# Layer norm of the feed-forward with w1 centred on chip, sums of h and h squared on four column strips, and roots spread over the partitions through HBM

## The reference

```python
h = shift_token(x)                       # features 64..127 come from the token before
q, k, v = split(h @ wqkv)                # 8 heads of 64
q, k = rotary(l2norm(q) * qs, l2norm(k) * ks)
x = x + local_attention(q, k, v) @ wo    # windows of 64 tokens, each looks at its own and the one before
h = shift_token(x)
mu = h.mean(-1); var = h.var(-1)
h = (h - mu) / sqrt(var + 1e-05) * lg + lb
a, g = split(h @ w1 + b1)                # 2 x 341
x = x + (a * gelu(g)) @ w2 + b2
```

## Time and profile before

| | value |
|---|---|
| median of 3 runs | 1300.65 us |
| profiled execution, span | 1302.3 us |
| PE busy | 1259.0 us, 97% |
| ACT busy | 1160.9 us, 89% |
| POOL busy | 1138.8 us, 87% |
| DVE busy | 1093.2 us, 84% |
| granted TensorE clock, mean | 0.999 of full |
| layer 0, attention loop | to about 530 us |
| layer 0, feed-forward and recurrence's gates | to about 690 us |
| layer 1, attention loop | to about 1180 us |
| layer 1, feed-forward and output | to the end |

### The profile page before, as it was taken

One profiled execution on the slowest core, in us unless ns is written; L12 is line 12 of the kernel. 1 busy time (PEld: TensorE's weight loads), 2 busy tenths in 40 slices (PEclk: granted clock), 3 DMA queues, 4 the chain that ended last, 5 costly groups with the idle time before them and its releaser, 6 DMA issues.

```text
span 1302.3 us, 38176 instructions
## 1 busy us (share of the span) xinstructions
PE 1259.0 (97%) x13795; PEld 1007.6 (77%) x13795; DVE 1093.2 (84%) x1883; ACT 1160.9 (89%) x3529; POOL 1138.8 (87%) x840
## 2 busy tenths in 40 slices
PE   7999999999999999899989999999999999999997
PEld 4778888888888887667657888888888888876776
DVE  7888888888888887689878898898888998874777
ACT  5889999999999999777778999999999999998886
POOL 5999999999999988378779999999999999994776
PEclk9999999999999999999999999999999999999999
DMA  5222222222222221010011222222222222110223
GB/s 168 54 63 63 62 62 63 62 63 65 68 66 67 55 62 47 17 54 1 1 29 39 47 46 46 46 47 46 50 48 59 47 46 46 39 38 25 72 75 97
DMA packets 59258, 70.04 MB, mean 54 GB/s; under 512 B 7232, under 2 KB 37376, under 8 KB 59072
## 3 DMA queue, kind: packets, MB, share of 16 engines
q1 hardware_dynamic: 59072, 67.61, 20.8%
HBM read 13.33 MB, written 4.19 MB: 13 GB/s over the span
## 4 chain that ended last, share of the span: by engine, by line
PE 71%; POOL 11%; DVE 6%; issue 6%; ACT 5%; DMA 0%; DVEq 0%; SPq 0%; ACTq 0%; POOLq 0%
PE ps L209 57%; PE ps L272 7%; POOL t L1293 5%; PE ps L285 3%; PE ps L282 3%; ACT P L674 2%; POOL P L1293 2%; POOL hxr L1293 2%; DVE t L1003 2%; POOL side L1323 1%; DVE t L1014 1%; DVE nm L1033 1%; DVE B L1074 1%; DMA norm<-X 0%; ACT sqk L648 0%
## 5 line engine op out<-in xcount | busy, mean ns | idle before, releaser
L674 ACT ACTIVATE P<-ps,nm 128x128 f32<-128x128 f32 x1024 | 363.4, 383 | 0.4
L209 PE MATMUL ps<-wqkv,hT 128*128 128x512 f32 x1152 | 330.1, 427 | 15.7 <-DVE t L1003 12.9
L1293 POOL TENSOR_TENSOR t<-t 128x1024 f32<-128x1024 f32 x128 | 307.0, 2398 | 26.1 <-DVE t L1003 24.3
L1293 POOL TENSOR_TENSOR P<-P,rden 128x512 f32<-128x512 f32 x256 | 289.9, 1143 | 19.3 <-DVE rden L1040 18.1
L209 PEld LDWEIGHTS ps<-wqkv,hT 128*128 128x128 f32 x1152 | 214.5, 188 | 95.8 <-issue 28.0
L1293 POOL TENSOR_TENSOR t<-t,rr 128x1024 f32<-128x1024 f32 x128 | 244.0, 1907 | 19.3 <-ACT rr L657 19.1
L674 ACT ACTIVATION_READ_ACCUMULATOR P<-ps,nm 128x1 f32 x1024 | 229.8, 224 | 0.0
L1014 DVE TENSOR_TENSOR t<-ps,tabl 128x512 f32<-128x512 f32 x256 | 164.1, 683 | 41.8 <-ACT sqk L648 40.6
L1293 POOL TENSOR_TENSOR hxr<-hxf,hxr 128x512 fp32r<-128x512 f32 (+1 forms) x93 | 129.0, 1413 | 71.6 <-ACT hxr L732 71.6
L664 ACT ACTIVATE PT<-ps 128x1024 f32<-128x1024 f32 x128 | 130.4, 1019 | 52.8 <-PE ps L272 51.7
L1033 DVE TENSOR_REDUCE nm<-ps 128x4 f32<-128x512 f32 x256 | 173.8, 681 | 3.9 <-PE ps L209 3.8
(11 more groups left out here) (142 smaller groups left out, 2545.3 us busy)
## 6 DMA issues: line engine op xcount, KB each, us to landing
Vs<-Vn SPq DMA_DIRECT2D x224, 128.0 KB, 2.4
side<-in_x SPq DMA_DIRECT2D x17, 256.0 KB, 3.0
A<-X SPq DMA_DIRECT2D x16, 256.0 KB, 2.5
norm<-X SPq DMA_DIRECT2D x32, 128.0 KB, 2.2
norm<-X SPq DMA_DIRECT2D x32, 127.8 KB, 2.4
hsh<-X SPq DMA_DIRECT2D x31, 128.0 KB, 2.3
hsh<-X SPq DMA_DIRECT2D x31, 127.8 KB, 2.4
oT<-in_x SPq DMA_DIRECT2D x15, 256.0 KB, 3.0
```

The source lines that it names most:

```text
L209: return e.matmul(o, lhsT, rhs, start=start, stop=stop, skip_group_check=True)
L674: k = act(P[:, g, :], ps[:, 3 + s, (g % 4) * 128:(g % 4 + 1) * 128], ACT.Exp, bias=nm[:, g:g + 1], accum_out=den[:, g:g + 1])
L1293: return e.tensor_tensor(o, a, b_, op)
```

## The change

- **Sums.** `mean`, `centre` and `var` are gone. ACT `square_h` squares the shifted block itself (hit 9). PE `sums` (hit 10, now between `sims` and `turn_p`; before, `var` stood after `turn_p`) makes sums of h and of h squared over the features with a 1/128 matrix of 32 columns: product j of four takes tokens 128j to 128j + 127 of both slots (256 columns) and writes to partitions 32j to 32j + 31. So four token groups lie on four groups of partitions, and each has 128 columns of mean and 128 of mean square.
- **Variance and root.** ACT `square_mean` (hit 10) squares the mean (128 columns), DVE `variance` (hit 10) takes the larger of mean square and squared mean and subtracts the latter (two operations of 128 columns), ACT `log_var` and `root_var` (hit 11, both layers) work on 128 columns.
- **Spreading.** SP `keep_roots` (hit 11) writes four partitions of roots, 128 numbers each, to an HBM tensor `rows`, and `spread_roots` (hit 12) reads that row of 512 back to all 128 partitions into B.
- **Scaling.** `scale_h` multiplies the uncentred h with the roots in B: on POOL in layer 0 (hit 14), on DVE in layer 1 (hit 13).
- **w1.** The mean is taken out of w1 instead: after its load, DVE `centre_w1` forms weight times w1 minus its mean over the features, in two halves of 341 columns, with the mean from PE `w1_mean` (a product with a matrix of weight/128), at i = 3 to 5. The split into two parts moves from i = 5 and 6 to i = 6 and 7.
- **Buffers.** `h2` exists twice (slots 0 and 2), `sq` lies between them.
- **Order of bank 2 in layer 1.** `rec_out` moves from hit 10 to hit 8, with `rec_gamma` (DVE) and `rec_square` (ACT), and `rec_sum` (DVE) from hit 12 to hit 10.
- **Last block.** Its `sums` stand at b = 1 of the feed-forward loop, after `down(0)`; logarithm, root and the two table loads move from b = 1 to b = 2; the multiply for block 15 moves to b = 4, for block 14 to b = 1 (layer 0, POOL) or 2 (layer 1, DVE).

```diff
+        slots = norm.rearrange("p (k n) -> p k n", k=3)
+        h2, sq = [norm[:, 0:L], norm[:, 2 * L:3 * L]], norm[:, L:2 * L]
+        msq, rt = norm[:, L:L + 128], norm[:, L + 128:L + 256]
...
-        avg = part.to_broadcast([128, 128])
+        avg = part.to_broadcast([128, 32])
...
+        rows = nc.dram_tensor("rows", (DEPTH * NB, L), F32, kind="Internal").ap()
...
+        def moments(m, bank):
+            first, second = ps[:, bank, 0:128], ps[:, bank, 128:256]
+            return (first, second) if m % 2 == 0 else (second, first)
...
-                if i in (3, 4):
-                    e.wait_ge(s_b1g, l + 1)
-                if (b := hit(i, 5)) is not None:
+                if i == 4:
+                    e.wait_ge(s_wc, 2 * l + 2)
+                elif (b := hit(i, 5)) is not None:
                     e.wait_ge(s_xadd, 2 * (l * NB + b) + 1)
                 elif (b := hit(i, 7)) is not None:
                     e.wait_ge(s_xadd, 2 * (l * NB + b) + 2)
-                elif (b := hit(i, 8)) is not None:
-                    e.wait_ge(s_hc, l * NB + b + 1)
                 elif (b := hit(i, 10)) is not None:
-                    e.wait_ge(s_rv, l * NB + b + 1)
+                    e.wait_ge(s_var, l * NB + b + 1)
+                elif l == 0 and (i == TURN[2] or 8 <= i <= 4 * NB - 8):
+                    e.wait_ge(s_x, 3 if i == TURN[2] else hit(i, -4) + 1)
+                elif l and (b := hit(i, 8)) is not None and b < NB - 2:
+                    e.wait_ge(s_osq, b + 1)
+                elif i > 4:
+                    side_free(l, i - 1)
             def turn_p(l, i):
...
-            def mean(l, b, bank):
-                e.wait_ge(s_h2, 32 * (l * NB + b + 1))
-                mm(ps[:, bank, :], avg, h2[:]).then_inc(s_mu, 1)
-            def var(l, b, bank):
-                e.wait_ge(s_sqh, l * NB + b + 1)
-                mm(ps[:, bank, :], avg, rsd[:]).then_inc(s_va, 1)
+            def sums(l, b, bank):
+                m = l * NB + b
+                e.wait_ge(s_h2, 32 * (m + 1))
+                e.wait_ge(s_sqh, m + 1)
+                for j in range(4):
+                    k = mm(ps[32 * j:32 * j + 32, bank, 0:256].rearrange("p (k n) -> p k n", k=2), avg,
+                           slots[:, m % 2:m % 2 + 2, j * 128:(j + 1) * 128])
+                k.then_inc(s_mom, 1)
+            def w1_mean(l, h):
+                if h == 0:
+                    e.wait_ge(s_gp, 1)
+                else:
+                    e.wait_ge(s_wc, 2 * l + 1)
+                mm(ps[:, 2, 8:8 + HID], gpart[l].to_broadcast([128, 128]), w1h[h]).then_inc(s_wm, 1)
...
                         ln_turn(1, 2)
-                    extra = False
-                    if l and (b := hit(i, 10)) is not None and b < NB - 2:
+                    if l and (b := hit(i, 8)) is not None and b < NB - 2:
                         side_free(l, i - 1)
                         rec_out(b)
-                        extra = True
...
+                    if (b := hit(i, 10)) is not None:
+                        side_free(l, i - 1)
+                        sums(l, b, 2)
                     if 0 <= i - 3 < NT:
                         turn_p(l, i - 3)
...
-                    if i >= 5:
-                        if not extra:
-                            side_free(l, i - 1)
-                        elif l == 0:
-                            if i > 7:
-                                e.wait_ge(s_x, hit(i, -4) + 1)
-                        elif hit(i, 10) is not None:
-                            e.wait_ge(s_osq, hit(i, 10) + 1)
+                        w1_mean(l, 0)
+                    if i == 4:
+                        w1_mean(l, 1)
                     if (b := hit(i, 5)) is not None:
...
-                    if (b := hit(i, 8)) is not None:
-                        mean(l, b, 2)
-                    if (b := hit(i, 10)) is not None:
-                        var(l, b, 2)
...
-            def log_var(l, b, bank):
+            def square_mean(l, b, bank):
                 m = l * NB + b
-                e.wait_ge(s_va, m + 1)
-                act(rsd[:], ps[:, bank, :], ACT.Ln, bias=eps_ln).then_inc(s_rv, 1)
+                e.wait_ge(s_mom, m + 1)
+                act(msq, moments(m, bank)[0], ACT.Square).then_inc(s_m2, 1)
+            def log_var(l, b):
+                m = l * NB + b
+                e.wait_ge(s_var, m + 1)
+                act(rt, rt, ACT.Ln, bias=eps_ln).then_inc(s_rv, 1)
             def root_var(l, b):
                 m = l * NB + b
                 e.wait_ge(s_rv, m + 1)
-                act(rsd[:], rsd[:], ACT.Exp, scale=-0.5).then_inc(s_rs, 1)
-            def square_hc(l, b):
+                act(rt, rt, ACT.Exp, scale=-0.5).then_inc(s_rs, 1)
+            def square_h(l, b):
                 m = l * NB + b
-                e.wait_ge(s_hc, m + 1)
+                e.wait_ge(s_h2, 32 * (m + 1))
+                if b == 0:
+                    e.wait_ge(s_wlo, 4 + l)
                 if m:
-                    e.wait_ge(s_hn, m)
-                act(rsd[:], sq[:], ACT.Square).then_inc(s_sqh, 1)
+                    e.wait_ge(s_row, 16 * m)
+                act(sq, h2[m % 2], ACT.Square).then_inc(s_sqh, 1)
...
-                        if (b := hit(i, 10)) is not None:
-                            square_hc(l, b)
+                        if (b := hit(i, 9)) is not None:
+                            square_h(l, b)
...
-                        if (b := hit(i, 12)) is not None:
-                            root_var(l, b)
                         for b in due(i, 5, {NB - 1: NT - 1}):
                             rec_root2(b)
                         if (b := hit(i, 9)) is not None:
-                            square_hc(l, b)
-                        for b in due(i, 10, {NB - 2: NT + 1, NB - 1: NT + 2}):
+                            square_h(l, b)
+                        for b in due(i, 8, {NB - 2: NT + 1, NB - 1: NT + 2}):
                             rec_square(b)
...
-                    if i == 5:
-                        e.wait_ge(s_w1, 16 * (l + 1))
-                        if l == 0:
-                            e.wait_ge(s_mask, 48)
-                        act(w1r[:, 0, :], w1, ACT.Copy, scale=lcol(l, 0)).then_inc(s_whi, 1)
-                    if i == (3 if l else 6):
+                    if i == 6:
+                        e.wait_ge(s_wc, 2 * l + 2)
+                        act(w1r[:, 0, :], w1, ACT.Copy).then_inc(s_whi, 1)
+                    if i == (3 if l else 7):
...
+                    if (b := hit(i, 10)) is not None:
+                        square_mean(l, b, 2)
                     if 0 <= i - 3 < NT:
                         keep_p(l, i - 3)
...
                     if b == 1:
+                        square_mean(l, NB - 1, 7)
+                    if b == 2:
                         e.preload_act_table_set(ATTN)
-                        log_var(l, NB - 1, 7)
+                        log_var(l, NB - 1)
                         root_var(l, NB - 1)
...
-            def centre(l, b, bank):
+            def variance(l, b, bank):
                 m = l * NB + b
-                e.wait_ge(s_mu, m + 1)
-                if m:
-                    e.wait_ge(s_hn, m)
-                e.tensor_tensor(sq[:], h2[:], ps[:, bank, :], ALU.subtract).then_inc(s_hc, 1)
-            def scale_hc(l, b):
-                m, hn = l * NB + b, seq(B, b)
-                e.wait_ge(s_rs, m + 1)
-                if l:
-                    e.wait_ge(s_hs, b + 1)
-                elif b >= NB - 2:
-                    e.wait_ge(s_wlo1, b - (NB - 2) + 1)
-                e.tensor_tensor(hn, sq[:], rsd[:], ALU.mult).then_inc(s_hn, 1)
+                both = moments(m, bank)[1]
+                e.wait_ge(s_m2, m + 1)
+                e.tensor_tensor(both, both, msq, ALU.max).then_inc(s_vmax, 1)
+                e.wait_ge(s_vmax, m + 1)
+                e.tensor_tensor(rt, both, msq, ALU.subtract).then_inc(s_var, 1)
+            def scale_h(b):
+                m = NB + b
+                e.wait_ge(s_rb, 16 * (m + 1))
+                e.tensor_tensor(seq(B, b), h2[m % 2], seq(B, b), ALU.mult).then_inc(s_hn[1], 1)
+            def centre_w1(l, h):
+                e.wait_ge(s_wm, 2 * l + h + 1)
+                e.scalar_tensor_tensor(w1h[h], w1h[h], lcol(l, 0), ps[:, 2, 8:8 + HID], ALU.mult, ALU.subtract).then_inc(s_wc, 1)
...
                         if (b := hit(i, 13)) is not None:
-                            scale_hc(l, b)
+                            scale_h(b)
...
                     if i == 4:
                         bias1(l)
+                        centre_w1(l, 0)
+                    if i == 5:
+                        centre_w1(l, 1)
...
+                    if (b := hit(i, 10)) is not None:
+                        variance(l, b, 2)
...
+                    if l == 0 and i == 2:
+                        e.wait_ge(s_mask, 48)
+                        ts1(gpart[0], lcol(0, 0), 1.0 / D, ALU.mult)
```

(31 more changed lines are left out.)

95 lines of the change are left out of this document (47 added, 48 removed).

## The result

The changed kernel takes 1321.03 us (median of 4 runs, 1319.58 to 1321.69), the kernel before, on the same chip, 1300.63. The ratio is 1.0143, 95% interval 1.0129 to 1.0157: 20 us slower, where 19 us faster was forecast. The profiled execution spans 1318.8 us, 16.5 more than before. The device time is 1.7 to 2.2 us above the span in every execution on record, so the profiled execution of the kernel before took some 1304 us (an estimate), more than its median; the medians are 20.4 apart.

A forecast was written before the change was run, and what follows sets the result against it. PE was taken to bound the kernel (busy 97%), with POOL and ACT close behind. Layer 0 10.5, layer 1 6.75, last blocks 4.4, less 2.5 for w1, make 19.2 us gained: 1281.5 us, range 1271 to 1300.

The forecast's parts named there:

- The output product of the recurrence, moved to hit 8: Layer 1: PE waits 0.3 us for the projection's second add to X; the layer still gains 0.45 us per block.
- POOL as the next bound: Attention stages: with PE shortened, POOL's work binds, 30.8 us per block in layer 0 and 30.7 in layer 1.
- POOL's multiply: Layer 0: the 512-column multiply by the root moves from DVE to POOL and adds 1.25 us per block there.
- 1.24 us wait for the rotation: Layer 0: POOL's wait per block goes, since without DVE's multiply the rotation can start 1.3 us earlier.
- PE's saving, 1.15 us a block: Both layers: mean and variance products of 1.74 us give way to 0.59 us of new work on PE.
- The mode change and the four strips: PE's four sums products on 32 output columns run side by side, 0.44 us, plus 0.15 for changing array shape.
- rival (a): The four sums products on 32 output columns do not run side by side on PE: 1301 us; chance 0.10.
- Layer 0: Attention stage: 0.7 us gained per block (bounds 0 and 0.9), times 15 blocks, 10.5 us.
- Last blocks: Between the stages: less PE waiting and shorter mean and variance work, 2.7 us in layer 0, 1.7 in layer 1.
- w1: Once per layer: two fp32 products and a bank wait cost 1.25 us, 2.5 in all (bounds 1 and 5).
- transfers: Per block SP's 2 KB write and 256 KB read, 6 us at most, covered by later tiles: cost nothing.
- (c): None of POOL's waits in layer 0 shrinks and the added multiply is paid in full: 1310.8 us; chance 0.10.

The follow-up runs named there:

- sums_late: The changed kernel with only the sums products moved behind the P transposes, ACT's square of the mean behind its exponentials, output product left at hit 8: 1313.26 us.
- order_undone: The changed kernel with the recurrence's output product back at hit 10 and the sums products behind the P transposes: 1297.17 us, ratio 0.9969.
- before_rec8: The kernel before with only layer 1's output product of the recurrence, and its gamma, square and sum steps, moved to hit 8: 1320.32 us, ratio 1.0144.
- rec_one: As sums_late, but only the first of four 128-column tiles of each recurrence output product is multiplied, two of eight products left: 1304.77 us, ratio 1.0038.
- comp_short: As sums_late, but ACT's square, DVE's gamma product and DVE's sum after the output product work on 8 of 128 columns per tile: 1313.24 us, ratio 1.0103.
- root_short_undone: As order_undone, but the two ACT steps of the root in the recurrence work on 8 of 512 columns: 1298.48 us, ratio 0.9989.
- pool_less: As order_undone, but POOL's multiply by the root in layer 0 and recurrence input multiply in layer 1 work on 8 of 512 columns: 1295.3 us, ratio 0.9962.

## Why the prediction was wrong, point by point

**The output product of the recurrence, moved to hit 8: the step that failed.** It was costed as PE's wait for the second X add, 0.3 us, with ACT at 30.0 us of work not concerned. Of that wait at most 0.2 us came: the product starts 2.47 us after the projection ahead of it (850.90 to 853.37), which takes 2.29 in the kernel before (861.12 to 863.41). The price was paid one engine further. PE's 0.9 to 1.0 us stands ahead of the turn of q and of attention, for which ACT waits in the tiles in which it has no extra work; before, it stood right behind the 2.04 us that ACT has extra. That cost 1.1 to 1.4 us a block (32.60 in sums_late against 31.52 in order_undone; 32.82 in before_rec8 against 31.41). Forecast for 15 blocks of layer 1: 6.75 us gained; measured: 20.1 lost. Rec_one shows that the time is PE's, comp_short that it is not the moved companions', root_short_undone that ACT's roots hid it in the old place.

**POOL as the next bound, from sums of work: failed.** POOL's multiply costs what was said (1.30 at 246.67 us against 1.25), and its 1.24 us wait for the rotation is gone:

```profile
242.32 2.40 POOL L1310 TENSOR_TENSOR t<-t 128x1024 f32<-128x1024 f32 x1
...
246.67 1.30 POOL L1310 TENSOR_TENSOR B<-norm,B 128x512 f32<-128x512 f32 x1
```

But taking that multiply away again moved nothing. What fits the runs is a loop over two engines: PT copy, eight exponentials and two copies on ACT, then masks, scores and P transposes on PE. ACT in a tile without extra work but the mean's square and the moments' root, order_undone:

```profile
861.78 1.03 ACT L678 ACTIVATE PT<-ps 128x1024 f32<-128x1024 f32 x1 [0.57 <-PE ps L285]
...
866.07 0.66 ACT L709 ACTIVATE qT<-ps 128x512 f32<-128x512 f32 x1
...
869.18 1.02 ACT L678 ACTIVATE PT<-ps 128x1024 f32<-128x1024 f32 x1
```

ACT works without a pause from 861.78 to the end of that qT copy, and PE from 866.79 (masks) to 869.15 (end of the P transposes). 7.4 us, and neither engine is busy throughout. In the kernel before the same tile took 7.30 us with the variance product in it on PE: both limits had about the same length there, and PE's 100% showed only one. A sum of work per engine can't show that. In layer 0 the loop is shown to be the limit of order_undone (31.01 to 30.30 with ACT's copy halved, nothing with POOL's work cut). In layer 1 halving that copy gave 0.22 us a block only, and what holds the rest stays open.

**PE's saving, 1.15 us a block: too large.** The mode change and the four strips were right: 861.67 to 862.24 in order_undone, 0.57 us against 0.59 and against 1.3 for 1,024 columns in a row (twice the 0.67 below), so they run side by side, and rival (a) is out. The products removed were sized at 0.87 by a difference against the output projection, taking a column to cost the same in both. The v and q/k projections by themselves take 2.29 us (877.33 to 879.62 in the kernel before), so the piece of 2.96 leaves 0.67 for a mean or variance product. So the strips save 2 x 0.67 - 0.57 = 0.8 us. By the stretches above PE's work in a layer 1 block fell a little less, from 31.4 to some 30.75.

The Trainium skill ("TensorEngine Tiling (Array Packing)", Key Properties) says that a change of tile mode drains the array. No row shows the drain by itself; whatever it costs here is within the 0.57 us.

**Layer 0: the forecast size came only in another order, and against the longer of two blocks.** Forecast were 0.7 us a block, a period of 31.0; the kernel as changed gives 31.43, since its strips stand ahead of the P transposes for which ACT waits. With the strips behind them it is 31.01. So the forecast overlooked the same thing again: what of PE's work stands ahead of the products that ACT waits for. The number 31.0 came from POOL's work (30.8), which is not its cause: pool_less left it unchanged.

The 31.70 to start from is not fixed either. before_rec8 has the layer 0 instructions of the kernel before, yet of the twelve blocks in its middle six take 31.7 us, five 30.9 and one 31.10. POOL and DVE in a shorter block and in a longer one:

```profile
229.51 2.50 POOL L1293 TENSOR_TENSOR P<-P,rden 128x512 f32<-128x512 f32 x2
229.90 1.22 DVE L1074 TENSOR_TENSOR B<-norm 128x512 f32<-128x512 f32 x1
234.12 2.41 POOL L1293 TENSOR_TENSOR t<-t 128x1024 f32<-128x1024 f32 x1 [0.24 <-DVE t L1003]
...
291.29 2.04 POOL L1293 TENSOR_TENSOR P<-P,rden 128x512 f32<-128x512 f32 x2
291.65 2.23 DVE L1074 TENSOR_TENSOR B<-norm 128x512 f32<-128x512 f32 x1
296.89 2.39 POOL L1293 TENSOR_TENSOR t<-t 128x1024 f32<-128x1024 f32 x1 [1.24 <-DVE t L1003]
```

Where two of POOL's multiplies of P take 2.5 us, DVE's multiply by the root beside them takes 1.2 and POOL's wait for the rotation is 0.24; where they take 2.05, DVE's takes 2.2 and the wait is 1.24. In the profile before all steady blocks were of the second kind. So the 1.24 us that the forecast removed can go without any change, and against 30.9 the 31.01 of order_undone gains nothing. Why a block turns out one way or the other is not shown.

**Last blocks, w1, transfers.** The last blocks were to give 4.4 us, w1 to cost 2.5. Between the last P transposes of layer 0 and the fifth tile of layer 1 nothing came (189.5 to 189.7), and the start seems to cost 0.4 instead of 1.25; over all runs here that stretch lies between 188.9 and 193.4 us and the start between 73.5 and 74.9, so terms of this size can't be read from two profiles. After layer 1 the changed kernel gains 2.1 us (forecast 1.7), order_undone nothing (its last P transposes start at 1172.25, its span is 1296.3): not a term that can be relied on. The transfers through HBM, 3.1 us each, cost nothing to be seen, as forecast.

**The rivals.** (c), slower at 1310.8 us, was on the right side for the wrong reason: POOL's waits did shrink (none of 1.24 us for the rotation is left). The true mechanism, a moved PE product uncovered on ACT, was among none of them, and the range ended at 1300. The forecast also took 1.65 us off the span to come to a median; since a device time lies above its span, that only says that the profile before was one of the longer executions.

## What to carry to other kernels

Where a loop is ordered by hand over several engines, look at each step between two fixed points on the second busiest engine, and not at sums of work alone. Here a PE product was free only where the engine that waits for PE's next result had something else to do: moving 0.95 us of it by two tiles cost more than removing 0.8 us per block could give. Put added work of the busiest engine behind all results that others wait for in that step; behind one of them gave back 0.3 of 1.3 us. And take a block's length from many blocks of more than one execution before costing what its waits are worth.

## What was not expected of the hardware

Eight fp32 records of 8 columns (wr,A, 847.43 to 848.35, 0.92 us) take as long as with 128 columns (853.37 to 854.36, 0.99, and 863.41 to 864.30, 0.89, in the kernel before). A narrower output did not make this product cheaper; fewer products did (rec_one). Each record has a weight load of its own (the page counts 13930 products and 13931 loads), which may be what sets its time; no run shows it.

The same DVE multiply of 512 columns (L1074) takes 1.20 to 1.22 us or 2.23 to 2.24 us in one execution of before_rec8, beside two POOL multiplies that take 2.5 us in the first case and 2.05 in the second: where the two engines multiply at the same time either DVE pays 1.0 us or POOL 0.45, and which it is can change from block to block.
